# GpSimd's row scatters of three batch pairs, issued without the waits between their groups of four

## Chip, cores, metric

The kernel runs on one core of one Trainium2 chip. Times are device microseconds of one execution. Three executions of the kernel before gave 701.67, 701.93 and 704.39 us, median 701.93 us. A separate execution was profiled; it took 702.97 us, and its profile spans 701.2 us.

## What is computed

Two transformer layers with adaptive layer norms on x of 8 x 512 x 128. Cut to what matters here:

```python
x = L0_attn_x                                   # (8, 512, 128)
h = layernorm(x) * (1 + ca) + sa
x = x + ga * linear_attention(h)                # 16 heads of 8
h = layernorm(x) * (1 + cb) + sb
x = x + gb * top2_moe(h)                        # 8 experts, 128 -> 512 -> 128, gelu, with residual and its own layer norm
h = layernorm(x) * (1 + ca1) + sa1              # second layer
x = x + ga1 * softmax_attention(h)              # 8 heads, dk 16
h = layernorm(x) * (1 + cb1) + sb1
x = x + gb1 * top1_moe(h)                       # 8 experts, 128 x 128
```

In `top2_moe` each token is sent to its two best experts; the two results are weighted and summed.

## The kernel before

The 8 batches are worked on as 4 pairs of 1024 tokens (pair 0 to pair 3), a pair lying in SBUF as 8 tiles of 128 tokens. The first expert layer sorts a pair's 2 x 1024 (token, expert) entries by expert into 23 tiles of 128 slots in DRAM (`xs`, in the trace `slots_in`), runs the experts tile by tile, writes the results to `yd` (`slots_out`), and gathers them back.

Each engine runs an order written out by hand, a list of steps `kind.pair.part` in ORDERS; engines meet through semaphores. A step that waits holds everything behind it in the same engine's list. The steps that matter:

- GpSimd (POOL), `bsc.i.j`, line 690: scatter j of pair i, four indirect DMAs of 128 rows of 512 bytes each from `z2` (the normalised tokens, in `bufb`) to `xs[i % 2]`. A pair has four such groups, 16 DMAs. Each DMA adds 16 to the semaphore `sc_out` (`b_scattered`) when it has landed. The first group waits for the slot numbers, which VectorE makes in `brk.i` (line 1148). Groups 1 to 3 of pairs 1 to 3 wait until all earlier groups of the pair have landed; in pair 0 they don't.
- POOL, `bga.i.j`, line 703: gather j of pair i, four indirect DMAs from `yd` to `yt`. Group 0 waits for the pair's stored results, each later group for the landing of the one before.
- POOL, line 654 (`bn1`, `bn3`): the power of -0.5 of a layer norm. VectorE makes its input and uses its result.
- SyncE (SP), `bxl.i.j`, line 530: loads four slot tiles from `xs` to `xg`. `bxl.i.0` waits for all 16 scatters of the pair. SP's list also has the expert weights (`bw`, line 521), the result stores (`byo`, line 540) and the loads of the second layer's stacks (`cto`, `cst`, lines 555 and 563).
- TensorE (PE), `bxt.i.j`, line 1500: transposes those tiles; `bh` (line 1507) and `by` (line 1515) are an expert's two matmuls; `btr` (line 1464) transposes `z2` for the expert choice.
- VectorE (DVE), `bn4.i`, line 984: writes pair i's normalised tokens into `z2`. There is one `z2`, so it waits for all scatters of pair i - 1. `bcm` (line 1154) sums what `bga` brought; `anm` is line 1056 to 1059; `cpv` (line 1196) writes the second layer's values.
- The second expert layer has its own scatter (`rsc`, line 726), of pairs 0 and 1 together.

The part of POOL's list around the scatters is:

```
an1.2.0 bsc.0.0 bn1.1.0 bsc.0.1 bsc.0.2 bsc.0.3 an1.3.0 ...
bn1.2.0 bsc.1.0 bsc.1.1 bsc.1.2 bsc.1.3 bn3.2.0 bga.0.0 bga.0.1 bga.0.2 bsc.2.0 bga.0.3 bsc.2.1 bn1.3.0
bsc.2.2 cn1.0.0 bsc.2.3 bn3.3.0 cn2.0.0 cn3.0.0 bga.1.0 bga.1.1 bga.1.2 bga.1.3 cpt.0.0 ...
bsc.3.0 bsc.3.1 bga.2.0 cpt.2.0 bsc.3.2 bsc.3.3 bga.2.1 bga.2.2 bga.2.3 cpt.3.0 ...
```

Of the kernel before, what the change touches and what calls it, by code (L numbers as in the profile page):

```python
# [259 lines left out]
def build(nc, io, out):  # L260
    ctx = ExitStack()
    with ctx:
# [339 lines left out]
        def _(p):  # L602
# [41 lines left out]
            for kind, i, j in ORDER["POOL"]:  # L644
# [33 lines left out]
                if kind == "bsc":  # L678
                    if j == 0:
                        p.wait_ge(b_pos, i + 1)  # L680
                        p.wait_ge(b_z, i + 1)
                        if i == 0:
                            p.wait_ge(zx, 32)
                        if i >= 2:
                            p.wait_ge(b_xt, TG * (i - 1))
                    elif i:
                        p.wait_ge(sc_out, 256 * i + 64 * j)
                    for x in range(4 * j, 4 * j + 4):
                        k, t = divmod(x, NT)
                        nc.gpsimd.indirect_dma_start(  # L690
                            xs[i % 2], bass.IndirectOffsetOnAxis(ap=posi[i][:, k, t:t + 1], axis=0),
                            z2[:, t, :], None).then_inc(sc_out, 16)
# [653 lines left out]
        def _(pe):  # L1346
# [10 lines left out]
            def keep_busy_aside(us, it):  # L1357

                _, gr, c = next((k for k in ORDER["PE"][ORDER["PE"].index(it):] if k[0] == "pv"), ("pv", len(values) // NC, 0))
                if c:  # L1360
                    for _ in range(int(us / .23)):
                        nc.tensor.matmul(bank(7), nothing, rows, start=False, stop=False)
                else:
                    if gr:
                        pe.wait_ge(c_ot, gr)
                    keep_busy(us, bank(7))
# [289 lines left out]
```

## Time and profile before

| | |
|---|---|
| median of three runs | 701.93 us (701.67 to 704.39) |
| the profiled execution | 702.97 us |
| its span | 701.2 us |
| PE busy | 612.6 us (87%) |
| DVE busy | 485.8 us (69%) |
| ACT busy | 390.8 us (56%) |
| POOL busy | 331.9 us (47%) |
| 64 scatters of the first expert layer on POOL (line 690) | 67.0 us busy, 75.2 us idle before them |
| 64 gathers on POOL (line 703) | 61.4 us busy, 58.7 us idle before them |
| 92 loads of an expert's weights | 514 KB each, 4.8 us from issue to landing |

No engine is busy throughout; at each place another wait ends last. A row of a time line below gives the start and the length of a piece of work, and in brackets how long its engine was idle before it and what ended that. The four pairs' scatters stand on POOL at 82.9 to 107.4 us, 151.7 to 181.5 us, 209.3 to 245.8 us and 333.8 to 364.7 us of the span. A DMA row on POOL is the time in which POOL makes the descriptors; the data land later.

### The profile page before, as it was taken

To read this page: it belongs to the slowest core of one execution; us is meant where nothing else is said; L and a number is where in the kernel's file an instruction comes from. 1 tells how busy PE (TensorE), PEld (TensorE's weight loads), DVE (VectorE), ACT (ScalarE), POOL (GpSimd) and SP (SyncE) were. 2 spreads that over 40 slices of the span, in tenths; PEclk is the share of its full clock that TensorE was granted. 3 is DMA by queue.
4 is the path that set the end of the run, shared out by engine and by line. 5 is a ranking of instruction groups with operands and counts; after the bars stand their busy time and mean duration, and the time that the engine had idled before them with its cause. 6 is when DMAs were issued, how large, how long until landed. Compare 5 with 4: busy or idle time off the path is not lost. (4 is left out here: it accounts for less than half of the span.)

```text
span 701.2 us, 11955 instructions
## 1 busy us (share of the span) xinstructions
PE 612.6 (87%) x3825; PEld 393.9 (56%) x3825; DVE 485.8 (69%) x1275; ACT 390.8 (56%) x866; POOL 331.9 (47%) x363
## 2 busy tenths in 40 slices
PE   7988996999799979778997999988889897999875
PEld 4656556988798878566425498532243333533232
DVE  5377975456365652578876862887988773889996
ACT  2443043797566746436886766667554565664420
POOL 5122284534647663552674441465655364148323
PEclk9998998999879989989999999999998999999998
DMA  8200224567579678497627687217210617411121
GB/s 336 98 1 0 78 93 147 194 228 244 177 220 333 238 240 282 151 315 229 221 102 221 205 281 243 78 43 192 55 43 1 163 61 206 150 44 33 31 60 30
DMA packets 47037, 106.40 MB, mean 152 GB/s; under 512 B 7056, under 2 KB 22224, under 8 KB 45440
## 3 DMA queue, kind: packets, MB, share of 16 engines
q1 hardware_dynamic: 41424, 94.82, 42.5%
q0 software_dynamic: 5120, 10.50, 4.6%
q8 instruction: 31, 0.51, 0.3%
q10 hardware_dynamic: 432, 0.34, 0.2%
q14 instruction: 30, 0.25, 0.1%
HBM read 80.26 MB, written 25.17 MB: 150 GB/s over the span
## 5 line engine op out<-in xcount | busy, mean ns | idle before, releaser
L891 ACT ACTIVATE bufa<-PS 128x512 f32<-128x512 f32 x256 | 139.4, 599 | 78.5 <-PE PS L1558 72.3
L1202 DVE TENSOR_REDUCE mxs<-PS 128x2 f32<-128x1024 f32 x128 | 151.0, 1218 | 31.2 <-PE PS L1542 30.6
L850 ACT ACTIVATE bufb<-PS,bufb 128x128 f32<-128x128 f32 x368 | 103.5, 380 | 45.8 <-PE PS L1507 45.5
L1507 PE MATMUL PS<-bufb 128*128 128x128 f32 x736 | 99.9, 286 | 12.2 <-DMA bufb<-in_experts_dram 6.1
L1507 PEld LDWEIGHTS PS<-bufb 128*128 128x128 f32 x736 | 93.6, 201 | 18.6 <-issue 7.9
L690 POOL DMA_INDIRECT slots_in<-bufb x64 | 67.0, 1047 | 75.2 <-DVE bufb L1148 40.8
L1515 PE MATMUL PS<-bufb 128*128 128x128 f32 x736 | 96.4, 280 | 0.8 <-ACT bufb L850 0.7
L1515 PEld LDWEIGHTS PS<-bufb 128*128 128x128 f32 x736 | 90.3, 195 | 4.3 <-ACT bufb L850 1.5
L1542 PE MATMUL PS<-stk 96*128 96x512 bf16 x256 | 76.4, 392 | 16.9 <-DVE mxs L1202 5.3
L703 POOL DMA_INDIRECT bufb<-slots_out,bufb x64 | 61.4, 960 | 58.7 <-DMA bufb<-slots_out,bufb 34.0
L1558 PE MATMUL PS<-stk 108*128 108x512 bf16 x256 | 81.6, 389 | 7.5 <-ACT bufa L891 6.4
L1568 PE MATMUL PS<-bufa,vv 128*32 128x512 f32 x512 | 69.3, 624 | 0.6 <-ACT bufa L898 0.4
L1558 PEld LDWEIGHTS PS<-stk 108*128 108x128 bf16 x256 | 22.2, 99 | 70.2 <-ACT bufa L891 39.6
L1542 PEld LDWEIGHTS PS<-stk 96*128 96x128 bf16 x256 | 21.2, 99 | 58.2 <-DVE mxs L1202 21.6
L1355 PE MATMUL PS<-identb 128*128 128x512 bf16 x187 | 46.5, 395 | 2.2 <-POOL dm L612 2.2
L654 POOL TENSOR_TENSOR rstd<-rstd,mhalf 128x8 f32<-128x8 f32 x12 | 20.5, 1705 | 44.1 <-DVE rstd L976 44.0
L842 ACT ACTIVATE bufb<-PS,cols 128x512 f32<-128x512 f32 (+1 forms) x24 | 18.3, 767 | 36.9 <-PE PS L1500 36.9
L1611 PE MATMUL PS<-bufb 128*128 128x512 f32 x64 | 32.1, 637 | 3.8 <-DVE bufb L1328 2.3
L1355 PEld LDWEIGHTS PS<-identb 128*128 128x128 bf16 x187 | 18.9, 102 | 22.0 <-issue 3.5
L1500 PE MATMUL PS<-identf,bufb 128*128 128x128 f32 x92 | 17.0, 319 | 11.8 <-DMA bufb<-slots_in 10.3
L1568 PEld LDWEIGHTS PS<-bufa,vv 128*32 128x32 f32 x512 | 11.7, 109 | 25.3 <-issue 19.9
L734 POOL DMA_INDIRECT bufb<-slots_out,bufb x16 | 15.5, 968 | 21.7 <-DMA slots_out<-bufb 17.1
(292 smaller groups left out, 980.4 us busy)
## 6 DMA issues: line engine op xcount, KB each, us to landing
bufb<-in_experts_dram SPq DMA_DIRECT2D x92, 514.0 KB, 4.8
stk<-split SPq DMA_DIRECT2D x48, 256.0 KB, 5.1
slots_out<-bufb SPq DMA_DIRECT2D x30, 256.0 KB, 3.1
bufb<-slots_in SPq DMA_DIRECT2D x25, 256.0 KB, 3.0
split<-terms SPq DMA_DIRECT2D x8, 768.0 KB, 3.8
slots_in<-hb SPq DMA_DIRECT2D x2, 1536.0 KB, 9.9
X<-in_x_dram SPq DMA_DIRECT2D x4, 512.0 KB, 6.7
out_dram<-X SPq DMA_DIRECT2D x6, 256.0 KB, 3.4
```

Source lines behind the costliest of these rows:

```text
L690: nc.gpsimd.indirect_dma_start(xs[i % 2], bass.IndirectOffsetOnAxis(ap=posi[i][:, k, t:t + 1], axis=0), z2[:, t, :], None).then_inc(sc_out ...
L703: nc.gpsimd.indirect_dma_start(yt[:, k, t, :], None, yd[i % 2], bass.IndirectOffsetOnAxis(ap=posi[i][:, k, t:t + 1], axis=0)).then_inc(ga_ ...
L850: last = nc.scalar.activation(hs[:, n % HR, fc, :], ps[:, P * fc:P * fc + P], ACT.Gelu_apprx_tanh, bias=ws[:, n % WR, F + fc:F + fc + 1])
L891: nc.scalar.activation(probs[:, i % PR, j, :], psum("s2", i, j), ACT.Exp, scale=DH1 ** -0.5)\
L1202: nc.vector.tensor_reduce(mxs[:, gr % 2, 2 * j:2 * j + 2, h], psum("s1", i, j).rearrange("p (c n) -> p c n", c=2), axis=AX.X, op=ALU.max)\
L1355: nc.tensor.matmul(place, identb[:, :], rows, start=True, stop=True)
L1507: last = nc.tensor.matmul(ps[:, P * fc:P * fc + P], ws[:, n % WR, P * fc:P * fc + P], xq[:, q % 2, P * x:P * x + P], start=True, stop=True)
L1515: last = nc.tensor.matmul(y, hs[:, n % HR, fc, :], ws[:, n % WR, W2AT + D * fc:W2AT + D * fc + D], start=(fc == 0), stop=(fc == FC - 1))
L1542: last = nc.tensor.matmul(ps[:, S * (c % 2):S * (c % 2) + S], qst[b % 2][0:KS, h, P * c:P * c + P], kst[b % 2][0:KS, h, :], start=True, st ...
L1558: nc.tensor.matmul(ps, kst[b % 2][0:KM, h, P * c:P * c + P], qst[b % 2][0:KM, h, :], start=True, stop=True).then_inc(c_s2x, 1)
L1568: last = nc.tensor.matmul(bank(7)[32 * hh:32 * hh + 32, :], vv[:, b % 3, j, 4 * k + hh, :], probs[:, n % PR, hh, :], start=(j == 0), stop= ...
L1611: last = nc.tensor.matmul(ps[:, 512 * e2:512 * e2 + 512], xTd[i % 2][:, P * j:P * j + P], expT[:, 4 * e2:4 * e2 + 4, :].rearrange("p e d - ...
```

## The change

The wait of groups 1 to 3 of a pair's scatter for the landing of the groups before is taken out for pairs 1 to 3. The waits of group 0, of the gathers and of the second expert layer's scatter stay.

```diff
@@ -683,8 +683,6 @@
                             p.wait_ge(zx, 32)
                         if i >= 2:
                             p.wait_ge(b_xt, TG * (i - 1))
-                    elif i:
-                        p.wait_ge(sc_out, 256 * i + 64 * j)
                     for x in range(4 * j, 4 * j + 4):
                         k, t = divmod(x, NT)
                         nc.gpsimd.indirect_dma_start(
```

No step changes its place on any engine. Pair 2's scatter on POOL, with the semaphores that a row waits for (`b_scattered` is `sc_out`; line 690 is the scatter, 703 the gather, 656 to 663 a layer norm), stands before as

```order
L690 DMA slots_in<-bufb 3072x128 [waits b_slots_turned,b_z,b_slots]
L690 DMA slots_in<-bufb 3072x128 x3
L703 DMA bufb<-slots_out,bufb 128x128 [waits b_gathered2]
L703 DMA bufb<-slots_out,bufb 128x128 x3
L690 DMA slots_in<-bufb 3072x128 [waits b_scattered]
L690 DMA slots_in<-bufb 3072x128 x3
L654 TENSOR_TENSOR rstd<-rstd,mhalf 128x8 [waits stats_ready_bn1]
L690 DMA slots_in<-bufb 3072x128 [waits b_scattered]
L690 DMA slots_in<-bufb 3072x128 x3
L656 TENSOR_TENSOR mom<-st 128x16 [waits stats_ready_cn1]
```

and afterwards, two line numbers lower, as

```order
L688 DMA slots_in<-bufb 3072x128 [waits b_slots_turned,b_z,b_slots]
L688 DMA slots_in<-bufb 3072x128 x3
L701 DMA bufb<-slots_out,bufb 128x128 [waits b_gathered2]
L701 DMA bufb<-slots_out,bufb 128x128 x3
L688 DMA slots_in<-bufb 3072x128 x4
L654 TENSOR_TENSOR rstd<-rstd,mhalf 128x8 [waits stats_ready_bn1]
L688 DMA slots_in<-bufb 3072x128 x4
L656 TENSOR_TENSOR mom<-st 128x16 [waits stats_ready_cn1]
```

The work between the groups (a gather, a power, a layer norm) has kept its place and its own waits.

## Rows read from the trace of the kernel before

**Rows 1.** What POOL waited for: total us, times, longest us.

```profile
POOL slots_in L690 <- DMA slots_in<-bufb: 18.3, 6, 4.7
```

**Rows 2.** POOL's time line, pair 0's scatter: first and last DMA.

```profile
82.89 1.22 POOL L690 DMA_INDIRECT slots_in<-bufb  x1 [16.35 <-DVE bufb L1148]
...
106.48 0.96 POOL L690 DMA_INDIRECT slots_in<-bufb  x1 [0.30 <-issue]
```

**Rows 3.** SP's queue, time line around four loads of slots (line 530).

```profile
108.71 1.29 SPq L530 DMA_DIRECT2D bufb<-slots_in  x3
...
180.18 2.07 SPq L540 DMA_DIRECT2D slots_out<-bufb  x2
182.79 1.27 SPq L530 DMA_DIRECT2D bufb<-slots_in  x3
...
247.05 0.81 SPq L530 DMA_DIRECT2D bufb<-slots_in  x2
```

**Rows 4.** POOL's time line, pair 1's scatter: groups 1 and 2, and what follows.

```profile
158.77 0.95 POOL L690 DMA_INDIRECT slots_in<-bufb  x1 [2.07 <-DMA slots_in<-bufb]
...
168.10 1.07 POOL L690 DMA_INDIRECT slots_in<-bufb  x1 [4.59 <-DMA slots_in<-bufb]
...
181.53 1.69 POOL L654 TENSOR_TENSOR rstd<-rstd,mhalf 128x8 f32<-128x8 f32 x1
```

**Rows 5.** The two stretches of pairs 0 and 1: busy by engine, PEclk, DMA share, GB/s.

```profile
82.90:108.70 25.80, 23.96 (x117) 13.85 (x115) 20.59 (x65) 7.15 (x14) 21.29 (x18) 1.00 0.33 121
151.60:182.80 31.20, 29.60 (x227) 27.07 (x226) 13.50 (x35) 24.03 (x60) 16.99 (x17) 1.00 0.67 221
```

**Rows 6.** DVE's time line at two places.

```profile
177.18 0.23 DVE L1050 TENSOR_SCALAR bufa<-bufa,PS 128x16 f32<-128x16 f32 x1
183.32 2.20 DVE L984 TENSOR_SCALAR bufb<-hb,mom,rstd 128x128 f32<-128x128 f32 x8 [5.90 <-DMA slots_in<-bufb]
...
382.96 0.61 DVE L1154 SCALAR_TENSOR_TENSOR bufb<-bufb,hb 128x128 f32<-128x128 f32 x2 [4.04 <-DMA bufb<-slots_out,bufb]
```

**Rows 7.** PE's time line: stalls after pairs 1, 2 and 3.

```profile
185.57 0.63 PE L1500 MATMUL PS<-identf,bufb 128*128 128x128 f32 x4 [2.23 <-DMA bufb<-slots_in]
187.21 1.97 PE L1464 MATMUL PS<-identf,bufb 128*128 128x128 f32 x8 [1.01 <-DVE bufa L1059]
...
249.86 1.09 PE L1500 MATMUL PS<-identf,bufb 128*128 128x128 f32 x4 [5.04 <-DMA bufb<-slots_in]
250.75 1.92 PE L1515 MATMUL PS<-bufb 128*128 128x128 f32 x8
...
384.76 1.03 PE L1542 MATMUL PS<-stk 96*128 96x512 bf16 x2 [3.90 <-DVE vv L1196]
```

**Rows 8.** POOL's time line, pair 2's scatter and the gather ahead of it.

```profile
205.86 0.96 POOL L703 DMA_INDIRECT bufb<-slots_out,bufb  x1 [0.30 <-issue]
209.30 1.13 POOL L690 DMA_INDIRECT slots_in<-bufb  x1 [2.48 <-DVE bufb L1148]
...
231.22 1.19 POOL L690 DMA_INDIRECT slots_in<-bufb  x1 [4.65 <-DMA slots_in<-bufb]
```

**Rows 9.** PE alone in three stretches: length, busy, PEclk, DMA share, GB/s.

```profile
187.20:189.00 1.80, 1.79 (x9) 0.50 0.89 340
...
249.90:252.00 2.10, 2.10 (x10) 0.50 0.82 270
...
384.70:387.70 3.00, 2.94 (x11) 0.50 0.21 64
```

**Rows 10.** POOL's time line, pair 3's scatter: groups 1 and 3.

```profile
340.35 0.96 POOL L690 DMA_INDIRECT slots_in<-bufb  x1 [1.61 <-DMA slots_in<-bufb]
...
359.95 0.96 POOL L690 DMA_INDIRECT slots_in<-bufb  x1 [1.53 <-DMA slots_in<-bufb]
```

**Rows 11.** Tile slots_out, 150 to 400 us: POOL's waits before gathers, total and times.

```profile
  DMA bufb<-slots_out,bufb: 28.6, 7
```

**Rows 12.** POOL's time line, the longest of these waits.

```profile
202.08 0.96 POOL L703 DMA_INDIRECT bufb<-slots_out,bufb  x1 [6.05 <-DMA bufb<-slots_out,bufb]
```

## The prediction

> **What bounds the kernel now.** I read first what POOL waits for, then POOL's time line at each pair's scatter, then who waits for the last scatter, and last what that costs PE, since PE is busy 87% of the span and at most places only a stall of PE, or of an engine that PE then waits for, moves the end.
>
> POOL waits six times for the landing of its own scatters, 18.3 us in all [rows 1]. Of these waits three are in pair 1 (2.07 us before group 1, 4.59 us before group 2, and one between them in size) [rows 4], one in pair 2 (4.65 us) [rows 8] and two in pair 3 (1.61 and 1.53 us) [rows 10]. In pair 2 the other two groups found the earlier ones landed: a gather and a layer norm stand between them. Each wait turns into the ordinary gap of 0.30 us between two DMAs [rows 2].
>
> Three things hang on a pair's last scatter: SP's load of the sorted slots, which PE then transposes; VectorE's `bn4` of the next pair, since there is one `z2`; and all that stands behind the scatter in POOL's list, gathers above all. PE shows it: 2.23 us of stall for loaded slots and 1.01 us for VectorE after pair 1, 5.04 us for loaded slots after pair 2, 3.90 us for VectorE's `cpv` after pair 3 [rows 7].
>
> **Do 16 scatters in a row land in time?** Pair 0 already issues them so: from 82.89 us to 106.48 + 0.96 = 107.44 us, 24.6 us with a power of another norm in between [rows 2], and SP's load that waits for all 16 goes at 108.71 us [rows 3], 1.3 us after the last issue. But the DMA engines were 0.33 busy there, and 0.67 in pair 1's stretch [rows 5]. The longest lag in pair 1 is the 4.59 us before group 2 [rows 4]. So I bound the lag of the last scatter by 1.3 and 4.6 us after the last issue. Pair 1's scatters would be issued 9 to 10 us sooner at best; its power, which stands at 181.53 us [rows 4], goes sooner by as much.
>
> **Term 1, pair 1.** VectorE's `bn4.2` began at 183.32 us. The row names the scatter as what ended the 5.90 us of waiting, but the power on POOL behind the scatter ran from 181.53 to 183.22 us [rows 4], so both held it; both move. VectorE is free from 177.41 us [rows 6]. With 16 issues of about 1.27 us from 151.7 us (or 24.6 us as in pair 0) the last ends at 172 to 176 us, and lands at 173 to 181 us; `bn4.2` (2.2 us) is done by 183.2 us even at the late end, which is about when PE has made what `anm.3` behind it reads. So the 1.01 us stall goes. The 2.23 us stall stays almost whole: SP issued its two result stores until 180.18 + 2.07 = 182.25 us and the slots' load at 182.79 us [rows 3], so only 0.54 us of it was the scatter; next comes the store of pair 0's results. Term 1 is 1.0 + 0.5 = 1.5 us, bounds 0 and 2.2 (below).
>
> **Term 2, pair 2.** The one wait is worth 4.65 - 0.30 = 4.35 us [rows 8], and nothing behind it in the list takes it back: the norm between groups 2 and 3 reads what VectorE made while group 2 was being issued. The scatter's start, 209.30 us, hung on slot numbers that follow PE, so it moves by term 1; it can't go before the gather ahead of it, whose last DMA ends at 205.86 + 0.96 us [rows 8], so no more than 2.2 us (that is the upper bound of term 1). The last landing, 247.05 us by SP's load [rows 3], moves by 4.35 + 1.5 = 5.85 us. PE stalled 5.04 us for it and itself arrives 1.5 us sooner, so it still stalls 5.04 - 4.35 = 0.7 us; PE gains 4.35 us here on top of term 1 (at most 5.04, at least 0 if the lag grows by as much as the wait was long). VectorE's `bn4.3` and POOL's second-layer norms stand behind the same scatter and move with it, so the attention that follows starts sooner as a whole. PE's next expert, `by.1.22`, ends pair 1's experts; its store starts the next gathers on POOL, so these move as well.
>
> **Term 3, pair 3.** POOL saves 1.61 + 1.53 - 0.60 = 2.54 us [rows 10]. The gather `bga.2` behind it ended 4.04 us of VectorE's waiting at 382.96 us [rows 6], with `cpv` behind that and PE's 3.90 us stall at 384.76 us behind `cpv` [rows 7]. I take 2.54 us; bounds 0 (the gather's own landings are late next) and 3.90 us (the gather gets out ahead of the load of the second layer's stacks).
>
> **Term 4, PE's clock.** In the stretches just after the stalls the granted clock is 0.50 of full speed, which is the lower of the two levels, 1.2 GHz: at 187.2, 249.9 and 384.7 us [rows 9]. The one at 187.2 us I leave out: it follows the 2.23 us stall, which stays, and what it could give is limited by the gather ahead of pair 2's scatter. After pair 2 the 1.09 and 1.92 us up to the end of `by.1.22` [rows 7] would be half as long at 2.4 GHz: 1.4 us. After pair 3, 3.00 us at half speed [rows 9] make 1.5 us. Whether a stall cut to 0.7 or 1.4 us still costs the clock, no row here decides. Bounds 0 and 2.9; I take the middle, 1.4 us.
>
> **Sum.** 1.5 + 4.35 + 2.54 + 1.4 = 9.8 us. From the profiled execution, 702.97 us, that leaves 693.2 us; the median of the runs was 701.93, 1.04 us lower, so 692.1 us. With all upper bounds, 2.2 + 5.04 + 3.90 + 2.9 = 14.0 us, 687.9 us.
>
> **What it adds.** Nothing is added; SP's list and all orders stay. The scatters fill POOL's queue without a pause, 1.05 MB in 21 to 25 us instead of 30 in pair 1. They share the engines with the weights; PE waits for weights at no place between 150 and 250 us, so I cost that at nothing; if the cover were gone, a weight load would be late by some part of its 4.8 us, once a pair.
>
> [...]
>
> **Rivals.**
>
> A. The landings are the limit, not the issue. The scatters then pile up in the queue, the last lands when it lands now, SP, VectorE and PE stay where they are: 701.9 us. For it: lags of up to 4.59 us in pair 1 against 1.3 us in pair 0. Against it: pair 0's sixteen in a row, and a DMA share of 0.67 that leaves a third free [rows 5]. This is also how the change would fail to do what it says: no wait, and no earlier landing.
>
> B. Only pair 2's wait counts. The gathers' own landings are late next after pairs 1 and 3, and the clock falls as now: 4.35 us, 697.6 us. For it: SP's row for pair 1 (0.54 us), and that the gathers keep their waits. Against it: PE's 3.90 us stall ends with a gather that is issued just behind pair 3's last group.
>
> C. Slower: the gathers pay. Their groups still wait for each other's landings, 28.6 us in seven waits in this part [rows 11], the longest 6.05 us [rows 12]. With PE stalling less, weights stream more densely and every one of these waits could become as long as the longest: 7 x 6.05 - 28.6 = 13.7 us on POOL, and VectorE waits for what they bring. This decides once it takes more than the 9.8 us of the sum; in full it gives 701.93 - 9.8 + 13.7 = 705.8 us. For it: these waits are long exactly where the DMA engines are full. Against it: weights are paced by PE's consumption, which grows by about 2% only.
>
> **How the numbers follow.** About 0.5% (3.5 us) is what a measurement of this kernel can tell from no change. My forecast, between 687.9 and 696, has a chance of 0.55; B (695.5 to 699.5) 0.20; A (within 1 us of before) 0.13; C 0.12, of which 0.07 beyond 705.4 us. Faster than 698.4 us: 0.55 and three quarters of B, rounded 0.71; slower than 705.4 us: 0.07; the rest, 0.22, within. The range runs from 687.0 us (all upper bounds, and the spread of the runs) to 701.5 us, which takes in B and a third of A and leaves C and the rest of A outside, some 0.2.
>
> **What would show it.** Right: in the profile after, 16 scatters per pair at 0.30 us gaps; `bn4.2` on VectorE near 177 to 181 us; PE's stall before pair 2's first transposes under 1 us instead of 5.04; its stall before the second batch's scores (3.90 us) shorter by 2.5 us or gone; the whole second half shifted by 8 to 12 us. Wrong: scatter DMAs on POOL that take longer than about 1 us each, or a last landing at the same place (A); PE's stalls gone but new ones before weights, or gathers' waits all near 6 us (C); a shift at 260 us that is gone by 441 us, where the last chain of waits begins.

## The result

The changed kernel took 695.82 us (median of 20 executions, 689.67 to 700.50), the kernel before beside it on the same chip 703.62 us (20 executions). The ratio is 0.9906, with a 95% interval of 0.9882 to 0.9929: of 701.93 us that is 6.6 us less (5.0 to 8.3), where 9.8 us were forecast. Ratios, here and in the table below, leave out executions that took over 1.5% longer than the fastest of their kernel (among them one of 1168.88 us of gathers_p1 and one of 1412.9 us of weights_first), so they are not quotients of the medians. The time lies inside the predicted range (687.0 to 701.5 us), 3.7 us above the predicted 692.1. The profiled execution of the changed kernel took 696.69 us (span 694.9), that of the kernel before 702.97 us (span 701.2).

### The profile after

In the changed kernel all line numbers from 688 on are two lower (in gathers_free below, where two more lines are out, those from 699 on are four lower). What POOL waits for (total us, times, longest us): the row of its own scatters [rows 1] is gone, and 61 of the 64 scatters have only the gap between two DMAs ahead of them. The gathers' waits are still there, a little longer (34.0 us in ten before, the longest 6.1).

```profile
POOL bufb L701 <- DMA bufb<-slots_out,bufb: 36.0, 10, 8.1
POOL slots_in L688 <- issue: 18.1, 61, 0.3
```

POOL's time line at pair 1 (start, length, in brackets the idle time before and what ended it): sixteen scatters from 151.11 us, the last issued by 172.41 us, and the power right behind.

```profile
151.11 1.25 POOL L688 DMA_INDIRECT slots_in<-bufb  x1 [8.91 <-DVE bufb L1146]
...
171.45 0.96 POOL L688 DMA_INDIRECT slots_in<-bufb  x1 [0.30 <-issue]
172.43 1.68 POOL L654 TENSOR_TENSOR rstd<-rstd,mhalf 128x8 f32<-128x8 f32 x1
```

VectorE's `bn4.2` and SP's loads of slots, to be read beside [rows 6] and [rows 3]: the scatters of pair 1 have landed at 177.67 us (before by 182.79, when SP's load went; `bn4.2` began at 183.32, behind POOL's power). But SP goes on at 181.81 only, since its two result stores stand ahead; pair 2's have landed at 241.54 (before 247.05).

```profile
177.67 2.14 DVE L982 TENSOR_SCALAR bufb<-hb,mom,rstd 128x128 f32<-128x128 f32 x8 [0.81 <-DMA slots_in<-bufb]
```

```profile
179.64 2.07 SPq L540 DMA_DIRECT2D slots_out<-bufb  x2
181.81 1.34 SPq L530 DMA_DIRECT2D bufb<-slots_in  x3
...
241.54 0.81 SPq L530 DMA_DIRECT2D bufb<-slots_in  x2
```

PE's time line at the places of [rows 7], and at a stall for expert weights:

```profile
184.71 0.63 PE L1498 MATMUL PS<-identf,bufb 128*128 128x128 f32 x4 [1.91 <-DMA bufb<-slots_in]
185.17 1.04 PE L1462 MATMUL PS<-identf,bufb 128*128 128x128 f32 x8
...
192.37 1.06 PE L1513 MATMUL PS<-bufb 128*128 128x128 f32 x8
...
244.27 1.09 PE L1498 MATMUL PS<-identf,bufb 128*128 128x128 f32 x4 [6.13 <-DMA bufb<-slots_in]
245.15 1.92 PE L1513 MATMUL PS<-bufb 128*128 128x128 f32 x8
...
295.42 2.05 PE L1505 MATMUL PS<-bufb 128*128 128x128 f32 x8 [6.61 <-DMA bufb<-in_experts_dram]
...
380.34 0.80 PE L1540 MATMUL PS<-stk 96*128 96x512 bf16 x2 [3.14 <-DVE vv L1194]
```

Two of these have no row among those of before; the same instructions stood in the kernel before at

```profile
199.96 1.09 PE L1515 MATMUL PS<-bufb 128*128 128x128 f32 x8
...
300.60 2.04 PE L1507 MATMUL PS<-bufb 128*128 128x128 f32 x8 [5.82 <-DMA bufb<-in_experts_dram]
```

So PE is ahead of before by 2.0 us at the transposes after pair 1 (187.21 to 185.17), by 7.6 us fifteen microseconds later (199.96 to 192.37), by 5.6 us after pair 2 (249.86 to 244.27), 5.2 us at the weights (300.60 to 295.42), 4.4 us after pair 3 (384.76 to 380.34), and 6.3 us at the end (701.2 to 694.9). Of each of these leads 0.5 us were there before the change could act: pair 1's first scatter began at 151.11 us, in the kernel before at 151.65. The gain is not a sum of three stalls: most of it is there after pair 2. To the stall after pair 3 PE comes 3.7 us ahead (384.76 - 3.90 = 380.86, and 380.34 - 3.14 = 377.20) and leaves it 4.4 us ahead, so the lead grows by 0.8 us there.

PE alone in some stretches (length, busy, granted clock as a share of full speed, DMA share, GB/s), before and then after. After pair 1 the clock stays at its upper level, 2.4 GHz; after pairs 2 and 3 (244.2 and 380.3 us, to be read beside [rows 9]) it falls to 1.2 GHz as before. From 310 to 335 us the changed kernel lost clock that the kernel before had kept (0.93 against 1.00), and with it most of the 1.5 us between 5.2 at the weights and 3.7 at the next stall. The 1.9 us that PE gains between 4.4 us and the end come where no wait was taken out, in part in a stretch where the one profiled execution of before had the lower clock (0.72 from 684 us, and 1.00 at about the same work afterwards, from 678 us).

```profile
184.00:200.00 16.00, 13.42 (x65) 0.57 0.74 240
310.00:335.00 25.00, 21.53 (x167) 1.00 0.79 261
684.00:690.00 6.00, 6.00 (x11) 0.72 0.19 44
```

```profile
184.00:200.00 16.00, 15.00 (x135) 1.00 0.90 294
240.00:256.00 16.00, 10.90 (x83) 0.79 0.79 251
244.20:246.40 2.20, 2.13 (x10) 0.50 0.84 252
310.00:335.00 25.00, 22.32 (x160) 0.93 0.61 185
380.30:383.30 3.00, 2.96 (x12) 0.55 0.25 66
678.00:684.00 6.00, 5.21 (x18) 1.00 0.09 21
```

Where did the 7.6 us go by pair 2? POOL's time line of the changed kernel, beside [rows 8]: pair 2's scatter stands right behind a gather and can't go before it, so it starts 2.24 us sooner (209.30 to 207.06) and not 7.6. Group 2 has lost its wait (231.22 to 224.10, 7.12 us sooner). Then the layer norm ahead of group 3 takes longer than before, where its last two steps had 0.20 and 1.67 us.

```profile
205.40 1.35 POOL L701 DMA_INDIRECT bufb<-slots_out,bufb  x1 [0.30 <-issue]
207.06 1.00 POOL L688 DMA_INDIRECT slots_in<-bufb  x1 [0.30 <-issue]
...
224.10 1.67 POOL L688 DMA_INDIRECT slots_in<-bufb  x1 [0.19 <-issue]
...
231.27 1.06 POOL L662 TENSOR_TENSOR rstd<-rstd,epst 128x8 f32<-128x8 f32 x1
232.41 2.65 POOL L663 TENSOR_TENSOR rstd<-rstd,mhalf 128x8 f32<-128x8 f32 x1
```

PE comes to pair 2's transposes 6.7 us sooner (249.86 - 5.04 = 244.82, and 244.27 - 6.13 = 238.14), the slots 5.5 us sooner. So its stall there has grown from 5.04 to 6.13 us.

### The profile page after: what moved, and what is told of

The parts are those of the page before. It is cut to its first block and busy times, and to the rows that moved or that the text cites. A ratio compares the mean times of both kernels' runs of the same rounds, so it can differ in the third digit from the quotient of the medians.

```text
span 694.9 us, 11955 instructions
## 1 busy us (share of the span) xinstructions
PE 602.8 (87%) x3825; PEld 385.3 (55%) x3825; DVE 484.6 (70%) x1275; ACT 390.7 (56%) x866; POOL 334.6 (48%) x363
## 5 line engine op out<-in xcount | busy, mean ns | idle before, releaser
L1505 PEld LDWEIGHTS PS<-bufb 128*128 128x128 f32 x736 | 90.5, 195 | 20.9 <-issue 9.0
L1513 PEld LDWEIGHTS PS<-bufb 128*128 128x128 f32 x736 | 91.3, 197 | 3.8 <-issue 1.4
L1353 PE MATMUL PS<-identb 128*128 128x512 bf16 x187 | 47.9, 404 | 2.2 <-POOL dm L612 2.2
L1609 PE MATMUL PS<-bufb 128*128 128x512 f32 x64 | 30.7, 610 | 4.1 <-DVE bufb L1312 2.2
```

The costliest lines, as they stand in the source:

```text
L1353: nc.tensor.matmul(place, identb[:, :], rows, start=True, stop=True)
L1505: last = nc.tensor.matmul(ps[:, P * fc:P * fc + P], ws[:, n % WR, P * fc:P * fc + P], xq[:, q % 2, P * x:P * x + P], start=True, stop=True)
L1513: last = nc.tensor.matmul(y, hs[:, n % HR, fc, :], ws[:, n % WR, W2AT + D * fc:W2AT + D * fc + D], start=(fc == 0), stop=(fc == FC - 1))
L1609: last = nc.tensor.matmul(ps[:, 512 * e2:512 * e2 + 512], xTd[i % 2][:, P * j:P * j + P], expT[:, 4 * e2:4 * e2 + 4, :].rearrange("p e d - ...
```

## The experiments

Every kernel was timed beside the kernel before; the ratios are to that one. Two kernels from different comparisons are set against each other by their ratios. For single pairs and for pairs of kernels that differ by little, the intervals, 0.002 to 0.006 to each side, are as wide as what is asked.

| kernel | waits that it has left, or its edit | median us | ratio | 95% interval |
|---|---|---|---|---|
| changed | gathers' | 695.82 | 0.9906 | 0.9882 to 0.9929 |
| p1_only | gathers', scatters' of pairs 2 and 3 | 702.45 | 0.9969 | 0.9938 to 1.0001 |
| p2_only | gathers', scatters' of pairs 1 and 3 | 702.00 | 0.9980 | 0.9947 to 1.0013 |
| p3_only | gathers', scatters' of pairs 1 and 2 | 699.20 | 0.9932 | 0.9899 to 0.9965 |
| p12 | gathers', scatters' of pair 3 | 696.53 | 0.9914 | 0.9878 to 0.9950 |
| gathers_free | none of the two | 687.13 | 0.9764 | 0.9725 to 0.9803 |
| gathers_only | scatters' | 692.51 | 0.9867 | 0.9823 to 0.9912 |
| gathers_p0 | gathers' of pairs 1 to 3 | 695.55 | 0.9890 | 0.9854 to 0.9926 |
| gathers_p1 | gathers' of pairs 0, 2, 3 | 690.55 | 0.9816 | 0.9768 to 0.9865 |
| gathers_p2 | gathers' of pairs 0, 1, 3 | 694.48 | 0.9888 | 0.9855 to 0.9921 |
| weights_first | as changed, two steps of SP's exchanged | 697.75 | 0.9925 | 0.9894 to 0.9956 |
| filler | as changed, PE kept busy in a stall | 697.53 | 0.9933 | 0.9903 to 0.9963 |
| rsc_free | as gathers_free, second layer's scatter too | 685.11 | 0.9720 | 0.9665 to 0.9775 |

### One pair at a time

```diff
-                    elif i:
+                    elif i and i != 1:      # p1_only; 2 and 3 in the others
                         p.wait_ge(sc_out, 256 * i + 64 * j)
```

> The waits between the scatter groups are out for pair 1 alone; pairs 2 and 3 keep theirs. My theory (each pair's wait counts only as far as the next wait on GpSimd lets it): PE's clock stays high after the first transposes, so PE stands about 7 us ahead at 200 us of the span, as in the changed kernel; but pair 2's scatter starts only when the gather ahead of it is issued, near 207 us instead of 209.3, so of the 7 us only 2.2 us or less are left at 250 us: PE's stall before pair 2's transposes becomes about 10 us, and the time is 1 to 2.5 us below the kernel before. Rival (the clock at 187 us is the main gain): 5 us or more below.

> The waits are out for pair 2 alone. My theory: GpSimd's 4.35 us reach PE, its stall before pair 2's transposes falls from 5.04 us to under 1.5 us, the clock isn't lost there, and the time is 4 to 6 us below the kernel before. Rival (the power and the sums of the norm on GpSimd that now fall beside VectorE's work run slower, some 2 us): 2 to 3 us below. Rival (the landings are the limit): no change.

> The waits are out for pair 3 alone. My theory after the changed kernel's trace: GpSimd issues its gather 2.5 us sooner, but the gather then lies in the loads of the second layer's stacks, whose place hangs on PE, and lands under 1 us sooner for VectorE; the time is 0 to 1 us below the kernel before. The forecast's own step: 2.5 us on the path and 1.5 us of clock, so 2.5 to 4 us below.

Pair 1 alone gave 2.2 us (an interval from 4.4 to nothing), pair 2 alone 1.4 us (3.7 less to 0.9 more), pair 3 alone 4.8 us (2.5 to 7.1). My expectation of the time was met for pair 1 and missed for the others (4 to 6 us for pair 2, at most 1 for pair 3). Pair 2 is not the one that counts; only pair 3's interval reaches what the whole change gives. In p1_only PE's time line shows where pair 1's gain goes: PE arrives 5.4 us sooner (239.39 and not 244.82 us), stalls 7.66 us for pair 2's slots, where it stalled 5.04 [rows 7], and is 2.8 us ahead behind them (249.86 to 247.05).

```profile
247.05 1.09 PE L1500 MATMUL PS<-identf,bufb 128*128 128x128 f32 x4 [7.66 <-DMA bufb<-slots_in]
```

p2_only was 4 to 5 us ahead in its profiled execution, but that one was the quickest of its twelve (696.44 us), so the runs decide there.

Pair 3 was then put back alone:

```diff
+                    elif i == 3:
+                        p.wait_ge(sc_out, 256 * i + 64 * j)
                     for x in range(4 * j, 4 * j + 4):
```

> The changed kernel with pair 3's waits put back: scatters of pairs 1 and 2 without waits. The changed kernel has 0.9906 of before, pair 3 alone 0.9932, pair 1 alone 0.9969, pair 2 alone 0.9980. Theory (the pairs add, and pair 3 is the largest part): 0.9969 x 0.9980 = 0.995, some 3.5 us below before. Rival (as the two profiled executions of before and after read: PE is 4.2 us ahead at 400 us, of which pair 3 made nothing, since SP's load of stacks and the gather behind it came late next): 0.991 to 0.992, no worse than the changed kernel.

The ratio is 0.9914, as the rival had it (the theory's 0.995 is the upper end of its interval), against the changed kernel's 0.9906: behind pairs 1 and 2, pair 3 adds some 0.6 us, though the intervals allow 3 us either way. PE's stall after pair 3, of p12 and then of p3_only, is to be read by its end. In p12 it is 3.81 us, 0.67 longer than in the changed kernel, but ends no later (380.10 and 380.34 us): PE only came to it sooner, since the changed kernel's execution had lost clock on the way. So at this place pair 3's saved issue brought nothing. In p3_only it is 2.17 us, 1.7 us shorter than before [rows 7].

```profile
380.10 1.03 PE L1542 MATMUL PS<-stk 96*128 96x512 bf16 x2 [3.81 <-DVE vv L1196]
```

```profile
388.85 0.61 PE L1542 MATMUL PS<-stk 96*128 96x512 bf16 x2 [2.17 <-DVE vv L1196]
```

In p3_only the matmul behind the stall took 0.61 us, and not 1.03 as before: the clock stayed up there, but was down again from 391 to 394 us (0.57). The profiled execution of p3_only took 705.15 us, longer than that of before. Why its runs alone gave as much as 4.8 us isn't settled; the 1.7 us of stall that the trace shows are less than the interval's lower end.

### The gathers' waits

```diff
-                    else:
-                        p.wait_ge(ga_in[j - 1], 64 * (i + 1))
```

This is taken out of the changed kernel (gathers_free), and out of the kernel before (gathers_only).

> The changed kernel, and the waits between the groups of the gathers out as well (group 0 keeps its wait for the stored results). It asks what is late next after the scatters. My theory: the gathers' waits hold pair 2's scatter (it would start near 202 instead of 207 us), so PE's 6.1 us stall shrinks by 3 us or more, and the split of the second layer's terms on GpSimd behind pair 1's gather comes up to 10 us sooner, so PE's 6.6 us stall for weights near 290 us shrinks too: 5 to 12 us below the changed kernel. Rival (the gathers are limited by their landings; sixteen in a row lie in the queue and push back the scatters and each other): within 2 us of the changed kernel, or slower.

> The kernel before with the gathers' waits between their groups taken out, and the scatters' waits kept: the other half of the kernel without either, which took 687.1 us (0.976 of before). Theory: the two kinds of wait cover each other in POOL's list, since pair 2's scatter is interleaved with gathers; whichever is left still holds the list. Scatters alone gave 6.6 us; without either it is about 17 us. If the two simply add, this kernel gains 17 - 6.6 = 10 us (ratio 0.985, some 693.5 us). If they cover each other, it gains clearly less than 10 us (0.99 or above), and the scatter's waits of 2 to 5 us are still there in the trace. Rival (the scatters' waits are the smaller evil once gathers run free, since sixteen scatters wait for one another only when the engines are full): it gains as much as the kernel without either, 0.976 to 0.979.

Without any of the two kinds of wait the kernel takes 687.13 us, 10 us below the changed kernel by the ratios, within the 5 to 12 that were expected. The gathers' waits alone are worth 1.3%, the scatters' alone 0.9%, and 0.9867 x 0.9906 = 0.977 is what both gave together, 0.9764. So over the whole kernel the medians say that the two add, against my theory that they cover each other (0.99 or above for gathers_only; its interval reaches 0.9912, so a part of it may stand). POOL's time line of gathers_free shows one place where they did cover each other: pair 2's scatter, which hung on the gather ahead, now waits for VectorE's slot numbers again and starts at 203.88 us, 5.4 us sooner than before [rows 8].

```profile
203.88 1.12 POOL L688 DMA_INDIRECT slots_in<-bufb  x1 [3.74 <-DVE bufb L1144]
```

PE's stalls of gathers_free: 2.15 us for pair 2's slots (6.13 in the changed kernel); after pair 3 it no longer waits for VectorE's `cpv`, but 3.16 us for the maxima that VectorE makes for the softmax.

```profile
241.31 0.94 PE L1496 MATMUL PS<-identf,bufb 128*128 128x128 f32 x4 [2.15 <-DMA bufb<-slots_in]
...
369.38 0.38 PE L1544 MATMUL PS<-identb,mxt 128*12 128x128 bf16 x4 [3.16 <-DVE mxt L1210]
```

### Which pair's gathers

```diff
-                    else:
+                    elif i:                 # gathers_p0; i != 1, i != 2 in the others
                         p.wait_ge(ga_in[j - 1], 64 * (i + 1))
```

> The changed kernel with the waits between the gathers' groups taken out for pair 0 alone (steps bga.0.1 to bga.0.3). These stand ahead of pair 2's scatter in POOL's list. Theory: they took back what pair 1 gained (pair 2's scatter began at 207.06 us, only 2.24 us sooner, where PE was 7.6 us ahead). With them out pair 2's scatter begins up to 5 us sooner, its last landing and PE's 6.13 us stall before pair 2's transposes by the same, 3 to 5 us of the time: ratio to the kernel before 0.984 to 0.987 where the changed kernel has 0.9906. Rival (PE's stalls before weights at 295 us and pair 3 decide, behind the gathers of pair 1): the start moves, and PE's stall at 295 us takes it back; ratio 0.989 to 0.992.

> The changed kernel with the waits between the gathers' groups taken out for pair 1 alone (steps bga.1.1 to bga.1.3). In POOL's list cpt.0.0 stands behind them, SP's store cto.0.0 waits for that, and the load of the weights bw.2.15 stands behind that store; PE stalled 6.61 us for these weights at 295 us in the changed kernel (5.82 before). Theory: that stall shrinks to under 2 us, and the time falls by 3 to 5 us, ratio to the kernel before 0.984 to 0.987. Rival (pair 0's gathers took the gain back): the stall shrinks, but PE is then held by the next thing, ratio 0.989 to 0.992.

> The changed kernel with the waits between the gathers' groups taken out for pair 2 alone (steps bga.2.1 to bga.2.3). The same for pair 1 alone gave 0.9816, for pair 0 alone 0.9890 (no clear difference from the changed kernel's 0.9906); for all four 0.9764. Theory: what pair 0 and pair 1 leave of the whole gain is pair 2's, since POOL waits 8.10 us in these gathers, and a gather ends VectorE's 3.32 us and with it PE's 3.14 us stall at 380 us in the changed kernel: 2 to 3.5 us, ratio 0.9855 to 0.988. Rival (that stall ends with the gather group 0, bga.2.0, whose waits stay): within 0.2% of the changed kernel.

Pair 0's gathers, my first suspect, give nothing that can be told (0.9890 against 0.9906). They were expected at 0.984 to 0.987. PE's time line of gathers_p0 shows where, in one execution, the gain goes: the stall for pair 2's slots shrinks from 6.13 to 2.66 us and ends 2.55 us sooner than in the changed kernel (244.27 to 241.72). But to the stall for weights at 294 us PE comes only 0.2 us sooner (288.60 and not 288.81): the lead is lost on the way, in part where the clock was lower (0.86 from 270 to 282 us, 1.00 in the changed kernel). Behind that stall 1.0 us is left (295.42 to 294.43).

```profile
241.72 1.09 PE L1498 MATMUL PS<-identf,bufb 128*128 128x128 f32 x4 [2.66 <-DMA bufb<-slots_in]
...
294.43 2.05 PE L1505 MATMUL PS<-bufb 128*128 128x128 f32 x8 [5.83 <-DMA bufb<-in_experts_dram]
```

Pair 1's give 0.9 points more than the change (0.9816), some 6 us, more than the 3 to 5 us of the theory. In gathers_p1 the expert that stalled 6.61 us for its weights (line 1505, here 16 matmuls in a row) runs on at once, and PE reaches the scores of the second layer at 296.58 us, where the changed kernel reached them at 303.16.

```profile
289.69 1.95 PE L1505 MATMUL PS<-bufb 128*128 128x128 f32 x16
...
296.58 1.02 PE L1540 MATMUL PS<-stk 96*128 96x512 bf16 x4 [1.36 <-DMA stk<-split]
```

Pair 2's (0.9888) can't be told from the changed kernel, as the rival had it: they take VectorE's `cpv` out of the way, and PE then stalls 3.18 us for the maxima instead of 3.14 us for `cpv`. Pair 3's gathers were not tried alone.

```profile
379.34 0.38 PE L1546 MATMUL PS<-identb,mxt 128*12 128x128 bf16 x4 [3.18 <-DVE mxt L1212]
```

### The weights, or the gathers behind them

```diff
-        bw.2.14 cto.0.0 bw.2.15 cst.0.0
+        bw.2.14 bw.2.15 cto.0.0 cst.0.0
```

> The changed kernel with two steps of SP's list exchanged: the load of the weights bw.2.15 ahead of the store cto.0.0, which waits for POOL's step behind the gathers of pair 1. PE stalled 6.61 us for these weights at 295 us. Theory: the stall for the weights goes, but cto.0.0 and the load of stacks behind it come as late as before, so PE's stall of 1.48 us for the stacks at 303 us grows by as much, to about 8 us, and the time stays within 0.2% of the changed kernel (0.989 to 0.9925): it is the gathers that hold the place, and the weights show only which of their followers is met first. Rival (the weights alone hold PE): the gain of the kernel with pair 1's gathers free, 5 to 6 us, ratio 0.982 to 0.984.

0.9925, the upper bound of the first theory, and outside the rival's (0.982 to 0.984). PE's time line, and VectorE's, show the row that comes next when the weights are there in time: the stall for weights is gone (289.34), and PE stalls 4.04 us for VectorE's step `bgb` (line 1121), which frees the bank that PE wants and stands on VectorE behind the sum of what pair 1's gathers bring (line 1152, 4.31 us of waiting for them). The stack of 303 us comes when it came. My expectation named the stack as the one that is met next; it was VectorE's list, hung on the same gathers.

```profile
289.34 1.95 PE L1505 MATMUL PS<-bufb 128*128 128x128 f32 x16
...
296.22 2.08 PE L1531 MATMUL PS<-wqkv,xTa 128*128 128x128 f32 x8 [4.04 <-DVE wa L1121]
...
303.09 1.02 PE L1540 MATMUL PS<-stk 96*128 96x512 bf16 x4 [1.61 <-DMA stk<-split]
```

```profile
288.06 2.15 DVE L1152 SCALAR_TENSOR_TENSOR bufb<-bufb,hb 128x128 f32<-128x128 f32 x2 [4.31 <-DMA bufb<-slots_out,bufb]
...
294.96 1.20 DVE L1121 TENSOR_TENSOR wa<-wa,PS 128x1024 f32<-128x1024 f32 x1
```

### The clock after a stall

```diff
-        bh.1.21@2 bh.1.22@1 by.1.20@2 bxt.2.0@0 by.1.21
+        bh.1.21@2 bh.1.22@1 by.1.20@2 bxt.2.0@0~55 by.1.21
```

The mark makes PE compute products that nobody reads, ahead of pair 2's transposes.

> The changed kernel with PE computing unread products (some 5.3 us of matmuls into a free bank) where it stalled 6.13 us for pair 2's slots, at 238 to 244 us; nothing else is changed. Theory of the clock term: the granted clock, which fell to half at 240.7 us for the work that follows, stays at full speed there, and the time falls by 1 to 2.5 us (ratio to the kernel before 0.987 to 0.989 where the changed kernel has 0.9906). Rival (the clock is a draw of the whole execution, not of this stall: another kernel without a change in pair 1 had a third of the low stretch that the profile of before shows after pair 1): the low stretch moves to another place, the mean granted clock over the runs stays at 0.961 to 0.962, and the ratio within 0.2% of the changed kernel's.

The clock did what was wanted and the time did not. PE's time line and one stretch (as above) of this kernel: the filler stands in the stall, the granted clock is 1.00 where the changed kernel had 0.79, and the two steps after the stall take 0.63 and 1.06 us, not 1.09 and 1.92.

```profile
237.49 5.13 PE L1353 MATMUL PS<-identb 128*128 128x512 bf16 x23
243.64 0.63 PE L1498 MATMUL PS<-identf,bufb 128*128 128x128 f32 x4 [1.02 <-DMA bufb<-slots_in]
244.10 1.06 PE L1513 MATMUL PS<-bufb 128*128 128x128 f32 x8
...
246.92 1.13 PE L1505 MATMUL PS<-bufb 128*128 128x128 f32 x8 [1.32 <-DMA bufb<-in_experts_dram]
```

```profile
240.00:256.00 16.00, 12.82 (x101) 1.00 0.80 259
```

Then PE stalls 1.32 us for weights, and again at 295 and 304 us for what the gathers of pair 1 hold. The ratio, 0.9933 (0.9903 to 0.9963), is not better than the changed kernel's, and the theory's 0.987 to 0.989 lies outside the interval. The rival's clock did not come either: the mean over the runs is 0.966, not 0.961 to 0.962.

### The second layer's scatter

```diff
-                    else:
-                        p.wait_ge(r_sc, 64 * j)
```

> The kernel without any wait between groups of the first expert layer's scatters and gathers (0.9764 of before, 687.1 us), with the same taken from the second expert layer's scatter (rsc.1.1 to rsc.1.3). In the changed kernel's profile POOL waits there for its own landings. Theory: these waits are short and that scatter starts on slot numbers made by VectorE; PE has softmax attention of other pairs to work on meanwhile: 0 to 2 us, ratio 0.9735 to 0.977. Rival (the scatter ahead of the second expert layer is on the path as in the first): 3 to 5 us, 0.969 to 0.972.

0.9720 (0.9665 to 0.9775) against 0.9764 (0.9725 to 0.9803): the intervals overlap, so this step can't be told from nothing. What it removes is small, as POOL's waits in gathers_free show:

```profile
POOL slots_in L722 <- DMA slots_in<-bufb: 3.1, 2, 1.5
```

Both kernels beat the change; 685 to 687 us is the best that was found.

## Why the prediction was right, and where it was not

**Sixteen in a row land sooner.** Right, and rival A falls as a whole: the landings are not where they were. Pair 1's scatters had landed by 177.67 us and not 182.79; pair 2's by 241.54 and not 247.05. `bn4.2` was forecast near 177 to 181 us and came at 177.67. But A held in part: the lag behind the last issue in pair 1, 177.67 - 172.41 = 5.3 us, is above the 4.6 us that I took as its bound, so that of the 9.1 us by which the issue ended sooner (181.51 to 172.41) 5.1 us reached the landing. The Trainium skill ("DMA: Bandwidth & Descriptors", section "Issuing engines are not separate DMA queues") says that DMAs initiated by several engines run on the same 16 DMA engines, so that initiating them on several engines at once saves the sequencer's time only, which no run here tries. It does not speak of waits between the DMAs of one engine; with these out, the landings came 5.1 us sooner at pair 1 and 5.5 us at pair 2.

**Term 1, pair 1 (1.5 us, bounds 0 and 2.2).** The bound was right, the value too low. The two stalls went as forecast (no stall in place of the 1.01 us, 1.91 us in place of 2.23). What PE gains there can reach pair 2 by no more than the gather allows, I had worked out, and pair 2's scatter moved by 2.24 us. But I left out the clock at 187 us, because the 2.23 us stall ahead of it stays. It stays (1.91 us), and yet the clock did not fall: the 1.01 us stall behind it is gone, and the granted clock of the stretch went from 0.57 to 1.00. In ten profiles without pair 1's waits it is 0.89 to 1.00; in four with them 0.57, 0.65, 0.58 and 0.89, the last being p2_only, where the stall of 1.01 us happened to be missing. In all fourteen the low clock goes with that stall; that the stall is its cause is read from these rows, no run changed the clock alone at this place. So PE is 7.6 us ahead fifteen microseconds later instead of 2.0. What counts at pair 2 is when the slots come, and these came 5.5 us sooner; the rest of the lead went into waiting for them.

**Term 2, pair 2 (4.35 us).** The sum of terms 1 and 2 was 5.85 us at this place; PE was 5.59 us ahead there and SP's load 5.51. That is the part of the forecast that was met, and in part by luck, since errors of both signs stand in it and 0.5 us of it were there before. Group 2 came 7.12 us sooner and not 5.85: its wait went as forecast (224.10 us, no wait), and the start moved by 2.24 and not 1.5. Then 1.06 + 2.65 - 0.20 - 1.67 = 1.84 us of it were lost again in the layer norm behind, which I had costed at nothing. And a stall of 0.7 us was forecast where 6.13 us remained, since PE came sooner than I let it: the stall's length was no measure of the gain, its end was.

**Term 3, pair 3 (2.54 us).** The step that failed. The scatters' last landing came 5.69 us sooner (SP's load, 366.01 to 360.32), but PE was only 4.4 us ahead at its stall behind the pair, and 3.7 us of that it had brought along. Of my two bounds the case lies near the lower one: VectorE's wait there still ends with the gather's own landing, now at 378.55 us (382.96 before, [rows 6]). The group that brings it was issued 6.7 us sooner and landed 4.4 us sooner. Its landing follows the loads of the second layer's stacks: these stand in SP's list behind a load of slots that waits for PE's transposes (365.80 us, before 369.45), and so come sooner by PE's own lead. p12, with pair 3's waits, shows it: there the group was issued 2.3 us later than in the changed kernel, SP's last load of the stacks was out at the same time (370.01 and 369.99 us), and POOL's wait for the group ended at the same time (378.54 and 378.78). In the ten profiles with this wait it ends 7.3 to 9.0 us after that load. POOL's first DMA of the group, before, in p12 and after:

```profile
372.67 0.95 POOL L703 DMA_INDIRECT bufb<-slots_out,bufb  x1 [2.86 <-DMA bufb<-slots_out,bufb]
```

```profile
368.25 0.95 POOL L703 DMA_INDIRECT bufb<-slots_out,bufb  x1 [3.05 <-DMA bufb<-slots_out,bufb]
```

```profile
365.96 0.95 POOL L701 DMA_INDIRECT bufb<-slots_out,bufb  x1 [1.84 <-DMA bufb<-slots_out,bufb]
```

VectorE's row for what it brings, in the changed kernel:

```profile
378.55 0.61 DVE L1152 SCALAR_TENSOR_TENSOR bufb<-bufb,hb 128x128 f32<-128x128 f32 x2 [3.32 <-DMA bufb<-slots_out,bufb]
```

By the runs of p12 the term is 0.6 us in the changed kernel (3 us either way), by the end of PE's stall nothing; alone it was 4.8 us by the runs, for a reason that stays open.

**Term 4, the clock (1.4 us).** Mis-sized the other way at each place: next to nothing after pairs 2 and 3, where the stretches read 0.50 before and 0.50 and 0.55 after, and a great deal after pair 1, where I had put nothing. The filler shows that to hold the clock up after pair 2 would not have brought the 1.4 us: weights and gathers are late next.

**The shift at 260 us and after.** It was to stay; 5.6 us at pair 2 were 4.4 at 380 us, where 8 to 12 had been forecast for the whole second half. The 6.61 us stall for weights (5.82 before) is where the second half meets pair 1's gathers, and gathers_p1 shows that these hold 6 us there.

**The rivals.** B (only pair 2's wait counts, 697.6 us) is nearer to the measured 695.8 than my own 692.1, and wrong in its mechanism: pair 2 alone gave 1.4 us, less than its 4.35. Its condition, that the gathers' landings are late next after pair 3, was the right half of it. C (the gathers pay) had the right culprit and the wrong price: their waits in this part grew from 28.6 us in seven [rows 11] to 30.5 in seven, not to 42, so at most 1.9 us were lost to them; they cap what is gained. With them out, the same scatters stand in a kernel 16 to 17 us below before.

So the time lies in the range by a sum whose first half was met and whose second half (terms 3 and 4, 3.9 of the 9.8 us) mostly was not. Of the signs named as right, the gaps of 0.30 us and `bn4.2` came; the stall under 1 us, the 3.90 us shorter by 2.5, and the shift of 8 to 12 us did not. The chance for a time below 698.4 us was added up a hundredth too high: 0.55 and three quarters of 0.20 make 0.70.

## What to carry to other kernels

Where a wait between groups of DMAs is taken out that nobody's data needs, look at once for the next of its kind in the same engine's list: at single places it holds back what the first gave up (pair 2's scatter stood behind a gather), and here it was worth more, 6.6 us for the scatters' waits and 17 us with the gathers'. For the worth of a stall, ask when its end can move, by everything that stands ahead in the releaser's own list, and not how long it is: PE's stall before pair 2 grew from 5.04 to 6.13 us while the kernel became faster. And before a late transfer is moved up, look who else waits for the same thing: with the weights loaded early, PE stalled for VectorE, on the same gathers.

## What the runs showed of the hardware

**Lag behind a burst.** The last of sixteen scatters had landed 1.3 us after its issue in pair 0 [rows 2, 3] and in pair 2 (240.26 to 241.54), and 5.3 us after it in pair 1, where sixteen were issued without a break. The DMA engines' mean share while they were issued and landed was 0.33 in pair 0 of the kernel before, 0.76 in pair 2 and 0.72 in pair 1 of the changed one, so the mean load alone does not make the difference; what does was not tried apart.

**POOL beside VectorE.** The two slow steps of POOL's norm lay on two VectorE products of 128 x 1024:

```profile
231.03 1.23 DVE L1080 TENSOR_TENSOR wa<-wa,modb 128x1024 f32<-128x1024 f32 x1
232.30 1.23 DVE L1081 TENSOR_TENSOR wa<-wa,modb 128x1024 f32<-128x1024 f32 x1
```

The step of 0.20 us ended at 232.33 us, just behind the first product (232.26), and the one of 1.67 us at 235.06, 1.53 us behind the second (233.53). The Trainium skill ("SBUF — State Buffer", section "Terms") has VectorE and GpSimd share a port pair that one of them holds for a whole instruction; these rows agree.

**Time and clock of one execution.** Over the 69 executions of the kernel before that the ratios of the other kernels use, the time falls by 0.44 us for each 0.001 of granted clock (correlation -0.80; clocks from 0.944 to 0.963). That is not a price: with the filler the mean clock was 0.966 against the changed kernel's 0.962, and the kernel was no faster. A shorter execution has the higher clock; which of the two leads was not separated. So one profile of a kernel can read several us off its runs, as that of p2_only did, and a lead of 1 or 2 us between two profiles need not be the work of an edit.
